# Attention's value product in three 16-bit passes instead of one 32-bit pass, with the split's lower parts on VectorE, and the router's small instructions spread between the large ones

## What is computed

```python
qkv = silu(x @ qkv_w.T)                        # 32 heads, q, k, v of 64 each
# block by block, 32 tokens at a time, with a state; the kernel does the same in one piece of 256 tokens:
#   y = ((q @ k.T) * decay, causal) @ v
attn = rmsnorm(y, norm_w)
x = layernorm(x + (sigmoid(x @ gate_w.T) * attn) @ out_w.T)
scores = sigmoid(x @ router_w)                 # 64 experts in 8 groups
# best two of each group -> best 4 groups -> best 6 experts; weights = scores / sum * 2.5
# an expert takes the first 48 tokens that chose it
y = sum over chosen experts of w * (silu(x @ wg[e]) * (x @ wu[e])) @ wd[e]
x = layernorm(x + y + shared_expert(x))
```

## Time and profile before

| | |
|---|---|
| median of 3 runs | 1414.53 us (1414.03 to 1414.83) |
| the profiled execution | 1412.41 us, its span 1410.4 us, granted clock 0.981 |
| busy share of the span | PE 95%, PEld 78%, DVE 63%, ACT 48%, POOL 26% |
| chain that ended last | PE 89%, DMA 4%, DVE 3% |

### The profile page before, as it was taken

The page is one execution under the profiler, slowest core; times in us unless marked ns, Lnnn a source line. Parts: engine busy times, 40 slices in busy tenths (PEclk is TensorE's granted clock), DMA queues, the critical chain, the costliest instruction groups (busy, mean ns, idle before and its releaser), DMA issues.

```text
span 1410.4 us, 36483 instructions
## 1 busy us (share of the span) xinstructions
PE 1345.9 (95%) x13995; PEld 1096.4 (78%) x13995; DVE 894.6 (63%) x2468; ACT 671.2 (48%) x1290; POOL 366.5 (26%) x422
## 2 busy tenths in 40 slices
PE   7999999999999999999999999999999999989960
PEld 5888888888888888888888888888888888865530
DVE  7856576666667575756576666667575756553337
ACT  8644454545454544445454545444444445433314
POOL 0212121212121122212121212121122222337754
PEclk9999999999999999999999999999999999999985
DMA  8500000000000000000000000000000000779957
GB/s 314 194 9 10 25 15 24 15 24 15 24 15 24 7 17 22 7 26 13 24 15 24 15 24 15 24 15 24 7 14 25 7 24 15 228 247 248 239 111 303
DMA packets 52962, 86.38 MB, mean 61 GB/s; under 512 B 6752, under 2 KB 32192, under 8 KB 52032
## 3 DMA queue, kind: packets, MB, share of 16 engines
q1 hardware_dynamic: 41728, 70.33, 14.7%
q0 software_dynamic: 5632, 8.26, 3.4%
q10 hardware_dynamic: 5568, 7.34, 1.5%
HBM read 60.08 MB, written 25.83 MB: 61 GB/s over the span
## 4 chain that ended last, share of the span: by engine, by line
PE 89%; DMA 4%; DVE 3%; issue 1%; POOL 1%; ACT 1%; SPq 0%; ACTq 0%; DVEq 0%; POOLq 0%
PE pA L467 25%; PE pB L467 23%; PE pC L543 13%; PE pO L557 12%; PE pS L529 10%; DMA sums<-sb_stage,sb_sidx 2%; PE pC L467 1%; PE pS L718 1%; DMA sb_W<-sums 1%; PE pC L577 1%; PE pB L701 1%; POOL sums L1292 0%; PE pS L701 0%; DVE sb_W L921 0%; DMA sb_stage<-gather_rows,sb_gidx 0%
## 5 line engine op out<-in xcount | busy, mean ns | idle before, releaser
L467 PE MATMUL pB<-sb_xh,sb_W 128*128 (+1 forms) x2048 | 349.9, 273 | 0.0
L1244 POOL TENSOR_TENSOR sb_fold<-sb_sq 128x256 f32<-128x256 f32 x128 | 111.5, 871 | 893.9 <-ACT sb_sq L801 893.9
L467 PE MATMUL pB<-sb_xl,sb_W 128*128 (+1 forms) x1024 | 279.3, 273 | 0.0
L467 PEld LDWEIGHTS pB<-sb_xh,sb_W 128*128 128x128 f16 x2048 | 200.5, 98 | 23.8 <-issue 0.2
L799 ACT ACTIVATE sb_yh<-sb_y 128x512 f16<-128x512 f32 x128 | 80.6, 630 | 286.4 <-DVE sb_y L937 286.4
L543 PE MATMUL pC<-sb_S,sb_v 128*64 128x256 f32 (+1 forms) x2048 | 194.7, 332 | 0.0
L945 DVE TENSOR_TENSOR sb_ql<-sb_q,sb_qh 128x512 f16<-128x512 f32 x128 | 88.0, 687 | 167.7 <-ACT sb_qh L775 164.3
L774 ACT ACTIVATE sb_q<-pA 128x512 f32<-128x512 f32 x128 | 76.4, 597 | 223.2 <-PE pA L467 223.1
L467 PE MATMUL pA<-sb_xh,sb_W 128*128 (+1 forms) x1024 | 175.9, 274 | 5.7 <-DVE sb_W L921 5.7
L467 PE MATMUL pA<-sb_W,sb_xh 128*128 128x256 f16 x1024 | 177.0, 275 | 2.1 <-ACT sb_qh L775 2.1
L557 PE MATMUL pO<-sb_Wo,sb_yh 128*128 128x256 f16 x1024 | 174.7, 273 | 1.0 <-DVE sb_yl L941 1.0
(11 more groups left out here) (210 smaller groups left out, 2315.5 us busy)
## 6 DMA issues: line engine op xcount, KB each, us to landing
sb_stage<-wprep SPq DMA_DIRECT2D x7, 1280.0 KB, 6.6
sb_W<-sums SPq DMA_DIRECT2D x16, 512.0 KB, 11.1
sb_W<-w_experts SPq DMA_DIRECT2D x16, 384.0 KB, 5.4
gather_rows<-sb_xr SPq DMA_DIRECT2D x16, 320.0 KB, 2.3
sb_D<-w_experts SPq DMA_DIRECT2D x12, 384.0 KB, 4.4
sb_xs<-xT SPq DMA_DIRECT2D x17, 256.0 KB, 2.9
sb_D<-decay SPq DMA_DIRECT2D x8, 512.0 KB, 7.6
sb_xn<-x SPq DMA_DIRECT2D x16, 256.0 KB, 3.0
```

Source lines behind the costliest of these rows:

```text
L467: last = nc.tensor.matmul(dst, a, m, start=(i == 0), stop=(i == len(terms) - 1), **kw)
L1244: nc.gpsimd.tensor_tensor(fold[:, :], sq[:, 0:T], sq[:, T:2 * T], ALU.add).then_inc(s_fold, 1)
```

## The change

**Attention.** `S` and `v32` are split like the other operands: ScalarE copies them to 16 bits (`high_S`, two instructions a step of 128x1024 and 128x512; `high_v`, 128x512), VectorE subtracts (`low_S`, 128x1536; `low_v`, 128x512), and `attention` takes 24 16-bit matmuls in place of the eight of 32 bits. `decayed` now goes by columns, 128x1024 and then 128x512, instead of four instructions.

**The order of a step.** TensorE: q, scores of g-1, k, attention of g-2, v, output of g-3, gate. The output is one step later; in the tail one more output product is left to do. The sums of squares, the router's product and the counts stand between scores and k, in steps 2, 4 and 6; the transposes after step 3's gate. VectorE: `decayed`, `low_v`, `gate`, `low_q`, `low_k`, `low_S`, `low_y`, with the router's instructions one by one between them; `Chain.link` no longer waits, and `ready` waits where the result is used.

**Moved to ScalarE:** the normalised rows (`normed`, with `nm1` computed by VectorE in `shift`), the sigmoid's affine step, the running counts and their carry. **GpSimd** adds all 512 columns of squares in one instruction, and the sum over the partitions takes both halves, four matmuls instead of two. The weights of the shared expert and the triangle are loaded into `xr`, the first three token tiles of the shared expert into `stage`.

```diff
             def attention(q, h):
-                pe.wait_ge(s_Sm, 2 * h + 2)
-                pe.wait_ge(s_ve, h + 1)
+                pe.wait_ge(s_Sl, h + 1)
+                pe.wait_ge(s_vl, h + 1)
                 wait(pe, s_sq, h)
+                wait(pe, s_y, h)
                 i = q % 2
+                products = [(vh[i], Sh), (vl[i], Sh), (vh[i], Sl)]
                 for u in range(2):
-                    for t in range(NT):
-                        for e in range(2):
-                            head = 2 * u + e
-                            last = nc.tensor.matmul(pC[64 * e:64 * e + 64, u * T + t * P:(u + 1) * T],
-                                                    v32[i][:, t, head * HD:(head + 1) * HD],
-                                                    S[:, head, 0:T] if t == 0 else S[:, head, T:T + P],
-                                                    start=(t == 0), stop=(t == NT - 1))
+                    for t, (a, z_) in enumerate(HALVES):
+                        for n, (v, s) in enumerate(products):
+                            for e in range(2):
+                                head = 2 * u + e
+                                last = nc.tensor.matmul(pC[64 * e:64 * e + 64, u * T + t * P:(u + 1) * T],
+                                                        v[:, t, head * HD:(head + 1) * HD], s[:, head, a:z_],
+                                                        start=(t == 0 and n == 0), stop=(t == NT - 1 and n == len(products) - 1))
...
+            def high_v(q, g):
+                act.wait_ge(s_ve, g + 1)
                 wait(act, s_C, g - 1)
+                nc.scalar.activation(vh[q % 2][:, :, :], v32[:, :, :], ACT.Copy).then_inc(s_vh, 1)
+
+            def high_S(h, i):
+                act.wait_ge(s_Sm, 2 * h + i + 1)
+                wait(act, s_C, h)
+                a, z_ = HALVES[i]
+                nc.scalar.activation(Sh[:, :, a:z_], S[:, :, a:z_], ACT.Copy).then_inc(s_Sh, 1)
...
+            def low_S(h):
+                dve.wait_ge(s_Sh, 2 * h + 2)
+                nc.vector.tensor_tensor(Sl[:, :, :], S[:, :, :], Sh[:, :, :], ALU.subtract).then_inc(s_Sl, 1)
+
+            def low_v(q, g):
+                dve.wait_ge(s_vh, g + 1)
+                wait(dve, s_C, g - 1)
+                nc.vector.tensor_tensor(vl[q % 2][:, :, :], v32[:, :, :], vh[q % 2][:, :, :], ALU.subtract).then_inc(s_vl, 1)
...
                 if has(g):
                     project_q(b, q, g)
-                    project_k(b, q, g)
                 if has(g - 1):
                     scores((q - 1) % NQ, g - 1)
+                if behind(b):
+                    if q == 2:
+                        sum_squares(b, g - 2)
+                    if q == 4:
+                        router(b)
+                    if q == 6:
+                        count(b, g - 2)
+                if has(g):
+                    project_k(b, q, g)
+                if tail and q == 1:
+                    output(b, (q - 3) % NQ, g - 3)
                 if has(g - 2):
                     bank_of_attention(b, q)
                     attention((q - 2) % NQ, g - 2)
...
                 if has(g):
                     project_v(b, q, g)
+                if has(g - 3) and not (tail and q == 1):
+                    output(b, (q - 3) % NQ, g - 3)
+                if has(g):
                     project_gate(b, q, g)
```

More of the change, by code:

```diff
@@ new lines, in router, with count @@
+            def router(b):
+                pe.wait_ge(s_x1T, b)
+                for t in range(NT):
+                    last = group(pC[:, t * EXP:(t + 1) * EXP],
+                                 [(x1T[:, c, t * P:(t + 1) * P], wr[:, c, :]) for c in range(NC)])
+                last.then_inc(s_r, 1)
+            def count(b, attended):
+                bank_free(attended)
+                pe.wait_ge(s_mask, b)
+                nc.tensor.matmul(pC[0:EXP, 0:T], mask[:, 0, :], triu[:, 0:T], start=True, stop=False)
+                nc.tensor.matmul(pC[0:EXP, P:T], mask[:, 1, :], triu[:, 0:P], start=False, stop=True).then_inc(s_cum, 1)
@@ L846, in step @@
                     split_weights(q + 1, (0, 1))
+                if behind(b) and not tail:
+                    if q == 4:
+                        evacuate_router(b)
+                    if q == 6:
+                        running_counts(b)
+                    if q == 7:
+                        carry_counts(b)
+                if has(g - 1):
+                    high_v((q - 1) % NQ, g - 1)
                 if has(g):
@@ L850, in step @@
                     split_weights(q + 1, (2,))
-                if has(g - 2):
-                    act_y(g - 2)
+                if behind(b) and q == 3:
+                    normed(b)
+                if has(g - 1):
+                    high_S(g - 1, 0)
+                    high_S(g - 1, 1)
                 if has(g):
                     act_v(q, g)
+                if has(g - 2):
+                    squares(g - 2)
+                    high_y(g - 2)
+                if has(g):
                     if early:
@@ L1071, in fill_slots, with search @@
-            def fill_slots(b):
-                chain = Chain(dve, s_find, FIND_LINKS * (b - 1), s_dve_passed)
-                chain.link(nc.vector.tensor_copy(carry[:, :], cumb[:, T - 1:T]))
-                chain.link(nc.vector.tensor_copy(foundf[:, :], found[:, :]))
-                chain.link(nc.vector.tensor_scalar(pen[:, :], foundf[:, :], float(T), FAR, ALU.is_ge, ALU.mult))
-                chain.link(nc.vector.scalar_tensor_tensor(cand[:, :], foundf[:, :], first[:, 0:1], pen[:, :], ALU.add, ALU.add))
+            def search(b, part):
+                if part == 0:
+                    wait_apart(dve, s_dve_passed, (s_cume, b))
+                for k in range(part * (CAP // 3), (part + 1) * (CAP // 3), 8):
+                    last = nc.vector.max_index(found[:, k:k + 8], vals[:, k:k + 8], cumb[:, :])
+                if part == 2:
+                    route["slots"] = Chain(dve, s_find, FIND_LINKS * (b - 1), s_dve_passed)
+                    route["slots"].link(last)
@@ L1114, in step @@
                     split_weights(q + 1, (2,))
[L1115 to L1120 removed]
+                if behind(b):
+                    if q == 4:
+                        route_best(b)
+                        route_group_scores(b)
+                    if q == 6:
+                        weigh_rows(b)
+                    if q == 7:
+                        slots_filled(b)
+                if has(g - 1):
+                    low_S(g - 1)
+                if behind(b):
+                    if q == 4:
+                        route_top_groups(b)
+                    if q == 6:
+                        search(b, 0)
                 if has(g - 2):
                     low_y(g - 2)
[L1123 to L1124 removed]
                 if early:
```

407 lines of the change are left out of this document (251 added, 156 removed).

## The result

The changed kernel takes 1446.14 us (median of 4 runs, 1445.06 to 1451.19) against 1414.68 us for the kernel before beside it (1414.03 to 1415.3): a ratio of 1.0224, 95% interval 1.0205 to 1.0244. The forecast was 1396, so the time is 50 us away, on the other side of no change. Its profiled execution took 1447.08 us, with a span of 1445.3.

The account below looks back on a forecast made before the run. TensorE's instruction stream was taken to bound the loop. From 1412.4: loop -24, VectorE +2.5, sequence 0 +1.5, tail +1.5 gave 1393.9; the runs' median, 2.1 above the profiled execution, made it 1396, range 1387 to 1414 us.

Parts of the forecast that it names:

- the iteration's sum: TensorE's loop: attention and switch save 0.24 us in each of 8 steps, router costs included, -1.6 an iteration, -24 in all.
- What would show it: List of signs: attention 1.05 to 1.15 us, k and v 1.42, TensorE without idle time in iterations of 74.0 to 74.4.
- Rival C: TensorE's 16-bit attention: weight loads bind the 128-column pairs, +0.31 us a step, 1436 us, slower; chance 0.09.
- Attention and the extra switch: TensorE's plain step: 16-bit attention 1.10 us for 1.45, -0.35; one more tiling switch, +0.11; step 8.97 against 9.21.
- Router: TensorE, per iteration: four 32-bit products for two in the sum over partitions, +0.4 us; counts share a switch, -0.1.
- VectorE: Loop: hidden behind TensorE in plain steps; late low_k in router steps and stretched low_y booked at +2.5 us in all.
- rival B: Loop, steps 5 to 7: VectorE binds and TensorE waits ahead of the scores, 1401 to 1414 us; chance 0.20.
- Sequence 0: First sequence: weights' splits bring VectorE to 9.4 us a step against 8.97, five times; booked +1.5 us (0 to +5).
- Tail: After the loop: one more output product and low_y waits, partly offset before the expert lists; +1.5 us (-2 to +5).

Follow-up runs that it names:

- the hinted kernel: The changed kernel with one added instruction, a hint naming the branch that closes TensorE's loop: 1401.31 us, 0.9907 of the kernel before.
- the order alone: The changed kernel with the back-branch hint and attention back in 32 bits, without the high and low parts of v and S: 1436.0 us, 1.0145 of before.

## Why the prediction was wrong

**The step that failed** is the iteration's sum, "-8 x 0.24 + 0.4 - 0.1 = -1.6, times 15". It prices what TensorE executes in a pass and takes the passes to follow each other as they did before, so the wait at the branch stands in it at nothing, without a reason. The 136 instructions that the new body has more are in the sum with their execution alone. They also made the body touch 8 blocks instead of 7, and that cost 44.1 us of fetching and lower clock, 3.15 at each of 14 branches. "What would show it" asked for TensorE without idle time in an iteration: that was the line to fail, and none of my rivals held the reason. Rival C's 1436 lies nearest to the measured 1446 by coincidence; its mechanism is refuted below. The sign of the forecast was wrong by the fetching alone: hinted, the same kernel is 0.9907 of before, near the forecast's 0.987.

**The terms, on the hinted kernel**, whose profile compares with the rows of before. Forecast 18.5 us less, measured 1410.4 - 1398.2 = 12.2:
- *Attention and the extra switch* were right to 0.02: step 8.97, attention 1.11 to 1.12, 0.055 between the pairs of 128 columns, k and v 1.42. The 34 to 35 us that separate the order alone from the whole are this term, less sequence 0. Timeline of the changed kernel:

```profile
457.34 0.22 PE L561 MATMUL pC<-sb_Sh,sb_vh 128*64 128x128 f16 x2
457.40 0.22 PE L561 MATMUL pC<-sb_Sh,sb_vl 128*64 128x128 f16 x2
457.45 0.22 PE L561 MATMUL pC<-sb_Sl,sb_vh 128*64 128x128 f16 x2
```

- *Rival C* (weight loads bind a 16-bit column tile) is refuted by the same rows. The loads of 64 columns are recorded with 106 to 111 ns each and the pairs start 0.055 apart, so the loads overlap. C reckoned with 0.107 a pair.
- *Router:* forecast +0.3 an iteration, measured 74.31 - 75.65 + 8 x 0.235 = +0.54. The sums of squares cost 0.54 more (step of 9.87 against 8.97, where before 9.57 stood against 9.21), the router's product behind its new neighbour 0.1, the counts -0.1.
- *VectorE* was booked at 2.5 us of stalls and cost none, although it is busier (68.1 us) than I forecast (about 60): rival B did not come true in the loop, hinted or not. Much of the surplus is `low_y`, at 1.25 us instead of 0.68 or 1.09: GpSimd's sum of squares was sized at 1.15 us from its nearest row and takes 2.23. Loop in all: -20.0 for a forecast -21.5.
- *Sequence 0:* +1.5 forecast, +4.6 measured (85.55 against 80.92 to the first q of sequence 1). The term was walked with undisturbed durations, 9.4 us a step; steps 1 to 5 took 9.0 to 10.9. The first step alone differs by up to 2 us between profiles; the seven behind it are 68.3 against 63.2, +5.2. +5.9 is what the 16-bit product's work costs there by the kernel with the order alone.
- *Tail:* +1.5 forecast, 207.0 against 203.9 us behind the last q: +3.2, of which 2.5 stand at the sums of squares (22.5 against 20.0). The tails of other kernels with the same order were 204 to 212 us, and that of the kernel before with the hint 207.3, so no more than the sums' part is shown: without the hint they come 22.3 us behind the last q in the changed kernel and 20.0 in the one before.

Together 18.5 - 1.5 - 3.1 - 1.7 = 12.2, and the fetches on top make the 1446.

**Left open:** which block gives way to which, since the packets carry no block number; why the changed kernel is 15 us faster on a block's boundary than unplaced, although it fetches 9 packets a pass at both places; and what of the tail's 3.2 us beyond the sums is the change's.

## What to carry to other kernels

A loop's body has a size as well as a duration: when a change splits instructions on an engine whose loop is long, count them, look at the instruction queue's row of the profile before, and expect a step at the size where packets begin to flow in the loop. Here that was the eighth block of 256 instructions, and the place of the loop's head in its block counts as well as the length. "issue" ahead of the first instruction behind a branch (2.17 us above) is the sign; a hint for the back branch, or writing the loop out, is the cheap test, and here also the cure as long as the body lies across 8 blocks (1446 to 1401 us; across 9, 1449). A wait in the profile that ends on some buffer tells who is late, not why: follow the chain a whole step before moving the instruction that it names.

## What the runs showed of the hardware

- Moving TensorE's loop within a 16 KB block, without touching its work, changed the time by 6% (1503.09 against 1414.51 us), and by about 1% in the changed kernel (1.0224 of before against 1.0106), which fetches its body anew at both places.
- A missed block leaves TensorE idle for 1.7 to 2.6 us, and in the changed kernel the granted clock of the 8.7 us behind it was 0.80 in eight of 14 passes: 3.15 us a branch in all there.
- A body of 1834 instructions that touches 8 blocks stays in place with the hint, and without the hint all of it is fetched anew in each pass (9 packets from branch to branch); across 9 blocks it is fetched anew with the hint too. With the hint the last packet of the first pass stays out, by its place the block behind the branch (5 packets instead of 6 in the kernel before), and TensorE waits 1.78 us once, behind the last pass. Across 9 blocks, with the hint, the packet ahead of the branch was there 2.0 us before the body's head (470.83 and 472.83 us).
- Straight code, the same body 15 times over, showed no wait of TensorE between 80 and 1200 us, with a packet of 16 KB every 10.6 us in the mean, one for 256 instructions.
- GpSimd beside VectorE: its addition of 512 columns took 2275 ns in the mean. Without these additions VectorE's `low_y`, which reads both inputs from SBUF, fell from 1.25 to 0.83 us in the mean, and to 0.68 where no work of GpSimd lay beside it.
